# A post-norm attention and gated feed-forward kernel: other rehearsed durations in the planner that orders its instructions

## What is computed

```python
x = layernorm(x + attention(x, w_attn, b_attn, w_proj, b_proj))   # one head, causal, softmax over 4096 keys
scores = x @ w_router; idx = top_k(scores, 0.75 * 4096)           # each sequence by itself
y = x with rows idx replaced by gelu(x[idx] @ w_block)
out = layernorm(x + y)
```

## Time and profile before

| | us |
|---|---|
| median of 3 runs (lowest, highest) | 967.45 (967.23, 970.24) |
| the profiled execution | 969.85 |
| its span, first to last instruction | 968.1 |

### The profile page before, as it was taken

One profiled execution on the slowest core, in us unless ns is written; L12 is line 12 of the kernel. 1 busy time (PEld: TensorE's weight loads), 2 busy tenths in 40 slices (PEclk: granted clock), 3 DMA queues, 4 the chain that ended last, 5 costly groups with the idle time before them and its releaser, 6 DMA issues.

```text
span 968.1 us, 15640 instructions
## 1 busy us (share of the span) xinstructions
PE 940.7 (97%) x5078; PEld 806.6 (83%) x5078; DVE 769.6 (79%) x1473; ACT 635.2 (66%) x993; POOL 274.3 (28%) x436
## 2 busy tenths in 40 slices
PE   9999999999999999999999999999999999998992
PEld 7889988888888888888888988888888888887771
DVE  4688996967966785789779989887899778568877
ACT  3566675764864585478555875686688558447985
POOL 3523124253042034513214253323203302111162
PEclk9999999999999999999999999999999999999996
DMA  6535344444253344567432533435777534336934
GB/s 190 175 123 171 110 142 121 121 130 141 76 164 104 104 151 158 165 213 228 153 126 82 186 111 108 164 94 180 241 237 251 172 100 131 119 100 219 314 131 174
DMA packets 85282, 149.53 MB, mean 154 GB/s; under 512 B 7761, under 2 KB 17618, under 8 KB 85202
## 3 DMA queue, kind: packets, MB, share of 16 engines
q1 hardware_dynamic: 85202, 148.54, 48.5%
HBM read 108.66 MB, written 39.85 MB: 153 GB/s over the span
## 4 chain that ended last, share of the span: by engine, by line
PE 93%; DVE 4%; issue 1%; ACT 1%; POOL 0%; ACTq 0%; DVEq 0%; POOLq 0%
PE sbank L514 37%; PE fbank L514 13%; PE obank L1048 11%; PE obank L1050 11%; PE obank L1049 11%; PE obank L1042 2%; PE obank L1044 2%; PE obank L1043 2%; PE fbank L1339 1%; PE fbank L1138 1%; PE mbank L946 1%; PE mbank L969 1%; DVE cmp L1502 1%; PE obank L554 1%; DVE tail L1751 0%
## 5 line engine op out<-in xcount | busy, mean ns | idle before, releaser
L514 PE MATMUL sbank<-qT,xT 128*128 128x512 f32 (+2 forms) x1728 | 413.2, 379 | 0.0
L514 PEld LDWEIGHTS sbank<-qT,xT 128*128 128x128 f32 x1728 | 306.4, 189 | 53.0 <-issue 0.3
L871 ACT COPY ring<-sbank 128x512 f32<-128x512 f32 (+3 forms) x288 | 157.5, 549 | 176.7 <-PE sbank L514 125.3
L1000 DVE TENSOR_TENSOR ring_lo<-ring,parts 128x1024 fp32r<-128x1024 f32 (+4 forms) x176 | 181.6, 1039 | 33.2 <-ACT parts L995 32.4
L1048 PE MATMUL obank<-ring_lo,vs 128*128 128x512 f32 x480 | 184.1, 384 | 4.1 <-ACT ot_sb L1107 1.6
L1050 PE MATMUL obank<-parts,vs 128*128 128x512 f32 x480 | 182.6, 380 | 0.0
L1049 PE MATMUL obank<-parts,vs 128*128 128x512 f32 x480 | 182.3, 380 | 0.0
L995 ACT CAST parts<-ring 128x1024 fp32r<-128x1024 f32 (+4 forms) x176 | 145.9, 834 | 52.4 <-PE obank L1050 39.7
L981 DVE TENSOR_TENSOR ring<-ring,mbank 128x1024 f32<-128x1024 f32 (+4 forms) x176 | 159.4, 946 | 9.4 <-PE mbank L969 9.4
L988 ACT ACTIVATE ring<-ring 128x1024 f32<-128x1024 f32 (+4 forms) x176 | 143.9, 845 | 24.7 <-DVE ring L981 24.4
L913 DVE TENSOR_TENSOR runmax<-ring,runmax 128x1024 f32<-128x1024 f32 x84 | 106.2, 1264 | 64.7 <-ACT ring L871 64.0
(11 more groups left out here) (222 smaller groups left out, 1204.7 us busy)
## 6 DMA issues: line engine op xcount, KB each, us to landing
vs<-v_scratch SPq DMA_DIRECT2D x288, 256.0 KB, 2.8
v_scratch<-vnew SPq DMA_DIRECT2D x30, 512.0 KB, 3.3
xres<-x SPq DMA_DIRECT2D x16, 512.0 KB, 4.7
out<-tail SPq DMA_DIRECT2D x32, 256.0 KB, 3.0
x_scratch<-xres SPq DMA_DIRECT2D x14, 512.0 KB, 3.1
y_scratch<-yb SPq DMA_DIRECT2D x14, 512.0 KB, 4.6
tail<-x_scratch SPq DMA_DIRECT2D x28, 256.0 KB, 3.5
tail<-y_scratch SPq DMA_DIRECT2D x28, 256.0 KB, 4.3
```

Of the source, the lines that this page charges most:

```text
L514: mm = eng.matmul(o, lhs(lh, k), rhs(rh, k), start=n == 0, stop=n == len(todo) - 1)
L871: act.copy(slot(n)[:, c0:], sbank[n % NSS][:, c0:]).then_inc(a_copy, 1)
L1000: dve.tensor_tensor(slots_lo(ns, c0), slots(ns, c0), f32(hi_of(u)), ALU.subtract).then_inc(v_lo, 1)
```

## The change

Five numbers of the rehearsal, and nothing else. A DMA takes 2.0 us and its bytes instead of 1.6 us and its bytes. A POOL instruction takes 0.35 us and one element in 460 per us, instead of 0.25 us and one in 457. A matmul of fp32r operands takes 0.11 us at least, instead of 0.06. A power takes 0.2 us for each element of its row, counted over all free dimensions, instead of 0.16 us for each element of the last dimension alone. Every instruction of the program stays; only their order on the engines may differ.

```diff
-DMA_US, DMA_BYTES_US, FIRST_BYTES_US = 1.6, 320e3, 250e3
+DMA_US, DMA_BYTES_US, FIRST_BYTES_US = 2.0, 320e3, 250e3
...
-         "pool": (.25, 1 / 457, .1), "sp": (.45, 0.0, 0.0)}
+         "pool": (.35, 1 / 460, .1), "sp": (.45, 0.0, 0.0)}
...
-        self.time += max(.22 if passes == 4 else .06, .0132 + self.per_element * passes * int(np.prod(out.shape[1:])))
+        least = .22 if passes == 4 else .11 if rhs.dtype == F32R else .06
+        self.time += max(least, .0132 + self.per_element * passes * int(np.prod(out.shape[1:])))
...
         if op == ALU.pow:
-            self.time += .16 * out.shape[-1]
+            self.time += .2 * int(np.prod(out.shape[1:]))
```

## The result

The changed kernel takes 972.34 us in the median of 11 runs (970.63 to 974.48), the kernel before 967.87 in 11 runs beside it (966.92 to 971.57). The ratio is 1.0036, with a 95% interval of 1.0022 to 1.0051: 3.5 us slower, a little beyond the 0.3% that I had called no change. The ratio goes by the means, 972.33 and 968.78. The medians lie 4.5 us apart, because before has six runs at 966.9 to 967.9 and five at 970.0 to 971.6. The profiled execution took 971.93 us, its span is 970.2.

A forecast was written before the change was run, and what follows sets the result against it. PE's work was taken to bound the kernel up to 928.7 us, then a chain on DVE. Gains of 0.5 and 0.5 against a loss of 1.0 left 969.85 us profiled, median 967.5, range 960.5 to 977.

The forecast's parts named there:

- The likeliest case: Whole kernel: no change beyond about 0.3%, 964.6 to 970.4 us, taking in C and D; chance 0.38.
- The sum: Profiled execution: 969.85 - 0.5 - 0.5 + 1.0 = 969.85 us, the median of after put at 967.5.
- What bounds the kernel: PE's work between 18 and 928.7 us, idle 6.3 us there; from 928.7 a chain on DVE.
- The lower clock's 1.7 us: PE at 886.6 to 890.3, behind two waits: nine matmuls at nearly the lower clock lose 1.7 us.
- The narrow matmuls: PE's 128-column outputs: rehearsed 6.8 us longer in all; 0.3 us of gain, taken as 0.5, at the twelfth group's maximum.
- POOL's additions: 95 additions on POOL, none on PE's way; new price not clearly nearer, small effect of the edit.
- A DMA's way and the router: Last group's router planned 0.5 to 0.7 us later; about 0.5 gained of PE's 0.89 us, router's wait under 1.0.
- The losses without a place: Idle spots of PE anywhere in the new order: +1.0 us, with a spread of some 3 us.
- Rival A: Fills slip behind the spread in up to five groups, 7 us slower: 974.5, up to 977 with the clock; chance 0.35.
- Rival D: Tail: DVE takes the last statistics ahead of the search's rounds, 969 to 970 us; inside the forecast's 0.38.
- Rival C: Whole kernel: the order hardly differs, nothing moves, 967.5 us; inside the forecast's 0.38.
- Rival B: Waits at router, last group's entrance and turns mostly go, 5 us faster: 962.5, at best 958; chance 0.27.

The follow-up runs named there:

- norms_first: The changed kernel with the last group's four normalizations moved in ACT's queue ahead of the seventh of the last scalings; median 972.06 us, ratio 1.0038.
- only_pow: The kernel before with the new price of powers alone; ratio 0.9992 (0.9976 to 1.0007).
- pow_act_tail: The kernel before with the powers' price alone changed, and ACT's queue from the first late cast on in the old order; 966.73 us, ratio 0.9978.
- sums_behind_reduce: The changed kernel with POOL's two subtractions waiting for DVE's third small step at the eighth group's maximum; 970.3 us, ratio 1.0025.
- both_mended: The changed kernel with POOL's two subtractions held behind DVE's small step and ACT's queue from the first late cast in the old order; 966.72 us, ratio 0.9979.
- narrow_mended: The kernel before with the narrow matmuls' price alone changed, plus the wait of POOL's two subtractions for DVE's small step; 973.5 us, ratio 1.0041.

## Why the prediction was right or wrong

**The range and the bound.** The range of 960.5 to 977 holds 972.3, but it is 16.5 us wide, and that says little for the mechanism. The likeliest case, within 0.3% or 964.6 to 970.4 us, was missed by little: 0.36%, with an interval that reaches down to 0.22%. The sum had a net of 0; what it lacked is 3.5 us.

**What bounds the kernel** held. PE's busy time is the same, all losses are waits of PE in the body or the chain behind 928, and each idle microsecond there is one of the total. The lower clock's 1.7 us for 3.4 us held too, but I had tied it to the two waits at the last group's entrance. norms_first has PE's order of the changed kernel and the same two waits of 1.64 and 1.41 us, and no stretch behind them; only_pow and pow_act_tail have both waits and a clock of 1.00 all the way to the last values matmul. Whether a stretch follows differs from one execution to the next, and so do its number and place: 0 to 3 ahead of the last values matmul.

**The narrow matmuls.** The 6.8 us of rehearsed time were right as arithmetic, against rows of 0.12 to 0.13 us. But "the new one not too early" was taken for a gain at the turns. The turns' waits did go (1.4 us), and the spread at the eighth group got 1.75. The step that failed is that a price nearer to the chip makes a better order: alone, this one costs 0.9%.

**POOL's additions.** "None is on PE's way" was wrong, and the two rows that could have told it were before me: 1.28 to 2.40 us for one form, and the router's first step of 1.50 us where the next took 0.42. The first I read as POOL being held up, the second I passed over. It goes the other way too: a DVE step of 0.16 us lasts as long as POOL's addition. The section "Key points" of the Trainium skill's "GPSIMD Engine Reference", which I had taken as a reason for a small effect of that price, names a contention of POOL with DVE instructions that have two SBUF inputs, and doesn't say who is held up. The two slow steps have two such inputs, and the traces agree: 1.14 and 1.18 us beside POOL, 0.17 and 0.16 without. Which small step meets an addition is decided by the order. The plan does let such steps exclude each other (`port`), the small ones too, but its times are not the chip's by then.

**A DMA's way and the router.** The sum had 0.5 us of gain here. The router's step came at 901.77 instead of 902.04 and waited 1.49 us instead of 1.44, PE behind it 1.61 instead of 0.89. I expected under 1.0. That gain didn't come. PE goes on 1.3 us behind the start of the low parts in both, 906.35 behind 905.02 and 906.61 behind 905.29; its wait is longer because PE reaches the place 1.0 us earlier, at 904.74 instead of 905.72.

**The losses without a place**, +1.0 in the sum: this is the term that was mis-sized. In the body they came out at 1.7 in the pair of profiles, but bodies of one order differ by 1 to 2 us between executions: 924.9 and 926.7 for the old, 926.6, 926.7 and 927.7 for the new, 924.5 and 925.8 for the new with the wait of POOL. By their means the body lost 1.2 us, and the wait gives back 1.9. The tail, 2.1 us, was not in it at all.

**Rival A** (slower, 974.5) had the direction and, in part, the place, PE at the spread. It was one group and not five, 1.75 us. Its mechanism is half of what happened: four transposes and twelve values matmuls had slipped behind the spread, and the 12 feed-forward matmuls now between turn and spread cover 2.02 us where before had 3.64. The other half, DVE beside POOL, it didn't have, and without that the shorter cover is enough (sums_behind_reduce). **Rival D** had the time at 969 to 970, 1.5 to 2.5 us for the tail; the size is right, its engine is not: DVE's statistics lie as before within 0.2 us a round, ACT's scalings do it. **Rival C** is out, the queues differ almost from their start. **Rival B** had nothing of its 5 us, which was added up too high besides: the waits that it lists come to 7.1 us and not 8, half of them and a little of the search to some 4. A slightly faster order exists, though: both_mended and pow_act_tail are at 0.998.

Still open is why the narrow price alone is so bad. Its mended version is at 1.0041, and its body of 929.9 had a stall that varies from execution to execution. How much of the +0.9% belongs to its order was not separated.

## What to carry to other kernels

In a kernel whose busiest engine is at 97%, a better price in a list planner isn't yet a better order. Of the four prices the narrow matmuls' and the DMA's came nearer to the trace, the powers' for the larger form, and POOL's was nearer in the mean of its additions and farther for its small steps; they gave +0.9, +0.4, -0.1 and +0.3% alone and +0.4% together. Judge a planner's change by the waits that its order opens, and mend those at their place (a wait that keeps a helper engine off a short critical step, a queue whose head isn't needed yet); two such edits gave back at least what the change had cost. Before believing a difference of 2 us between two profiles, take out the stretches at the lower clock.

## What the runs showed of the hardware that I had not expected

- A DVE step on 128x4 values out of SBUF takes 0.16 us alone and 1.09 to 1.22 beside a POOL subtraction of 128x512 that takes 1.25: it ends with POOL's. Taking POOL away by a wait brings back 0.16 to 0.17.
- Stretches of PE at the lower clock ahead of the search's end last 3.4 us in each trace and cost 1.7 us each; there were 0 to 4 of them in an execution. The same pair of waits, 1.65 and 1.41 us within 8 us, is followed by one in the changed kernel and not in norms_first, with the same order of PE.
- One store of 256 KB and the two reloads beside it took 6.9 to 7.1 us in one execution and 3.8 to 4.2 in another of the same order; the next reloads, issued behind the store's landing, came later by as much and more, and where a step that waits for one stood ahead of the scores' copies in ACT's queue this became 2.0 us of idle PE, in narrow_mended 3.6.
